# One signal of TensorE per half group, and an MLP that runs three groups ahead, in the edge loop of a graph kernel

## The reference

```python
h = silu(edge_feats @ A1 + b1)          # 8 -> 64
h = silu(h @ A2 + b2)                   # 64 -> 64
tpw = h @ A3                            # 64 -> 128, split in w0..w3
ss, vs = s[sender], v[sender]           # rows gathered from a table of the nodes
out_s0 = ss * y_s * w0;  out_s3 = (vs . y_v) / R3 * w3
out_v1 = ss * y_v * w1;  out_v2 = vs * y_s * w2
message = segment_sum(all of these, receiver) / 10
```

## Time and profile before

| what | us |
|---|---|
| median of 3 runs (2710.15 to 2735.73) | 2723.78 |
| the profiled execution | 2727.58 |
| its span on the core | 2725.8 |
| first `by_attributes` to the end of the last MLP wait (1380.98 to 2649.80) | 1268.8 |

### The profile page before, as it was taken

One profiled execution on the slowest core, in us unless ns is written; L12 is line 12 of the kernel. 1 busy time (PEld: TensorE's weight loads), 2 busy tenths in 40 slices (PEclk: granted clock), 3 DMA queues, 4 the chain that ended last, 5 costly groups with the idle time before them and its releaser, 6 DMA issues. The chain is left out here.

```text
span 2725.8 us, 32746 instructions
## 1 busy us (share of the span) xinstructions
PE 2131.8 (78%) x10250; PEld 1643.8 (60%) x10250; DVE 1571.8 (58%) x3518; ACT 1519.3 (56%) x4753; POOL 1585.9 (58%) x1672
## 2 busy tenths in 40 slices
PE   6488888888888888888768767777777777777776
PEld 4467767777776777767645545554554555555555
DVE  5356666666666665666735555554554555555557
ACT  3455454545455555454556656656666666666662
POOL 1666666666666666666166665665665665665660
PEclk8689999999999999898977888888887888888889
DMA  8666666666666666666111111111111111111111
GB/s 304 203 185 201 204 197 175 169 177 174 182 175 179 179 177 169 176 174 181 47 52 46 47 44 44 48 43 45 47 43 43 48 44 46 50 48 40 45 43 48
DMA packets 121049, 309.60 MB, mean 114 GB/s; under 512 B 29058, under 2 KB 42604, under 8 KB 120876
## 3 DMA queue, kind: packets, MB, share of 16 engines
q0 software_dynamic: 93264, 273.00, 36.0%
q1 hardware_dynamic: 27612, 34.51, 3.8%
HBM read 288.14 MB, written 19.26 MB: 113 GB/s over the span
## 5 line engine op out<-in xcount | busy, mean ns | idle before, releaser
L664 POOL DMA_INDIRECT sender<-table,src_index x832 | 785.8, 945 | 539.3 <-issue 286.9
L369 POOL DMA_INDIRECT shared<-gates,seq_index x833 | 789.1, 947 | 502.4 <-issue 221.2
L759 ACT ACTIVATE bank<-bank,attr 128x64 f32<-128x64 f32 x3328 | 702.3, 362 | 3.9 <-issue 3.6
L392 PE MATMUL bank<-ident,shared 128*128 128x128 f32 x3332 | 497.9, 294 | 230.7 <-DVE h_lo L467 155.2
L445 ACT ACTIVATE bank<-bank,bias 128x512 f32<-128x512 f32 (+1 forms) x663 | 401.1, 634 | 494.7 <-PE bank L404 322.9
L392 PEld LDWEIGHTS bank<-ident,shared 128*128 128x128 f32 x3332 | 425.1, 152 | 321.5 <-DVE h_lo L467 187.0
L713 PE MATMUL bank<-msg,select 128*128 128x256 f32 x1664 | 504.0, 455 | 2.1 <-DVE msg L806 2.1
L795 DVE TENSOR_TENSOR side<-sender,bank 128x192 f32<-128x192 f32 x416 | 147.0, 353 | 598.4 <-ACT bank L759 394.1
L698 PEld LDWEIGHTS bank<-a,h 64*128 64x128 f32 x1664 | 238.2, 218 | 378.9 <-issue 255.2
L698 PE MATMUL bank<-a,h 64*128 64x128 f32 x1664 | 281.1, 318 | 196.4 <-ACT bank L759 138.0
L713 PEld LDWEIGHTS bank<-msg,select 128*128 128x128 f32 x1664 | 356.8, 225 | 85.8 <-issue 9.3
(11 more groups left out here) (88 smaller groups left out, 2161.9 us busy)
## 6 DMA issues: line engine op xcount, KB each, us to landing
shared<-gates,seq_index POOLq DMA_INDIRECT x833
sender<-table,src_index POOLq DMA_INDIRECT x832
gates<-shared SPq DMA_DIRECT2D x49, 256.0 KB, 4.0
feats<-attr_in SPq DMA_DIRECT2D x13, 256.0 KB
x<-x_nodes_in SPq DMA_DIRECT2D x12, 256.0 KB
table<-up SPq DMA_DIRECT2D x12, 256.0 KB, 2.3
out<-x SPq DMA_DIRECT2D x12, 256.0 KB
shared<-x_t_in SPq DMA_DIRECT2D x3, 704.0 KB, 10.2
```

What stands on the lines that cost most here:

```text
L369: pool.indirect_dma_start(out=rows[:, k % SLOTS, j, :], out_offset=None, in_=t["gates"], in_offset=bass.IndirectOffsetOnAxis(ap=seq_index[ ...
L392: last = pe.matmul(bank[:, j * P:(j + 1) * P], rows[:, k % SLOTS, j, cols], ident[:], is_transpose=True, start=(j == 0), stop=False, skip_ ...
L664: pool.indirect_dma_start(out=sender[:, hg % 4, j, :], out_offset=None, in_=t["table"], in_offset=bass.IndirectOffsetOnAxis(ap=src_index[: ...
L759: last = act_e.activation(wy[:, j, :, k, :], w[:, 2 * i + j, :, min(k, 1), :], ACT.Copy, scale=attr[:, k, tile:tile + 1])
```

## The change

Six semaphores of PE become one, `e_pe`. PE adds to it once for each product in the lead-in, and once for each half of an iteration in the main loop; the values at which a reader may go on are worked out in four small functions. The MLP layers run three groups ahead in place of two, and `h2` has three buffers for that. The first layer moves behind the sums of its half, as the second one did already. The orders of ACT's loop and the waits of PE stay the same but for the three groups. In the diff below `mlp1`, `mlp2`, `mlp3` and `sum_receivers` return their last product and signal nothing themselves; the first block of changed lines is PE's, the second ACT's. DVE and SP are changed in their waits alone: `summed(hg - RING)` in `selections`, `summed` of the window's last half group in `add_window`, and `first_done(GROUP * (s - 1) - 1)` before a load of features.

```diff
+EARLY = 3
-        h2 = sb("h2", [P, 2, 512])
+        h2 = sb("h2", [P, EARLY, 512])
+        def first_done(g):
+            return 2 * g + 1 if g < EARLY else 2 * g + 2
+        def second_done(g):
+            return 2 * g + 2 if g < EARLY else 2 * g + 3
+        def weights_done(hg):
+            return 2 * EARLY + 1 if hg < 2 else 2 * EARLY + hg
+        def summed(hg):
+            return 2 * EARLY + hg + 3
...
-                    for g in range(2):
-                        mlp1(g)
-                        mlp2(g)
-                        mlp3(g)
+                    for g in range(EARLY):
+                        mlp1(g).then_inc(e_pe, 1)
+                        mlp2(g).then_inc(e_pe, 1)
+                    mlp3(0)
+                    mlp3(1).then_inc(e_pe, 1)
                     for g in range(NGROUP):
-                        mlp1(g + 2)
                         mlp3(2 * g + 2)
-                        sum_receivers(2 * g - 1)
-                        mlp2(g + 2)
+                        last = sum_receivers(2 * g - 1)
+                        last = mlp1(g + EARLY) or last
+                        last.then_inc(e_pe, 1)
                         mlp3(2 * g + 3)
-                        sum_receivers(2 * g)
-                    sum_receivers(NHALF - 1)
+                        last = sum_receivers(2 * g)
+                        last = mlp2(g + EARLY) or last
+                        last.then_inc(e_pe, 1)
+                    sum_receivers(NHALF - 1).then_inc(e_pe, 1)
...
-                        act_e.wait_ge(e_p1, g + 1)
-                        if g >= 2:
-                            act_e.wait_ge(e_p2, g - 1)
+                        act_e.wait_ge(e_pe, first_done(g))
-                        act_e.wait_ge(e_p2, g + 1)
-                        if g >= 2:
-                            act_e.wait_ge(e_w, 2 * (g - 1))
+                        act_e.wait_ge(e_pe, second_done(g))
+                        if g >= EARLY:
+                            act_e.wait_ge(e_pe, weights_done(2 * (g - EARLY) + 1))
-                        act_e.wait_ge(e_w, hg + 1)
+                        act_e.wait_ge(e_pe, weights_done(hg))
                     for g in range(NGROUP):
                         by_attributes(4 * g)
                         by_attributes(4 * g + 1)
-                        silu1(g + 2)
+                        silu1(g + EARLY)
                         by_attributes(4 * g + 2)
                         by_attributes(4 * g + 3)
-                        silu2(g + 2)
+                        silu2(g + EARLY)
```

More of the change, by code:

```diff
@@ L637, in build @@
         e_gather = [sem(f"e_gather{i}") for i in range(4)]
-        e_p1, e_h1, e_p2, e_h2, e_w, e_scaled = (sem(n) for n in ("e_p1", "e_h1", "e_p2", "e_h2", "e_w", "e_scaled"))
-        e_sel, e_msg, e_half, e_acc = (sem(n) for n in ("e_sel", "e_msg", "e_half", "e_acc"))
+        e_pe, e_h1, e_h2, e_scaled = (sem(n) for n in ("e_pe", "e_h1", "e_h2", "e_scaled"))
+        e_sel, e_msg, e_acc = (sem(n) for n in ("e_sel", "e_msg", "e_acc"))
         e_side, e_free, e_next = (sem(n) for n in ("e_side", "e_free", "e_next"))
-        e_sems = [e_rel, e_turn, *e_feats, *e_gather, e_p1, e_h1, e_p2, e_h2, e_w, e_scaled,
-                  e_sel, e_msg, e_half, e_acc, e_side, e_free, e_next]
+        e_sems = [e_rel, e_turn, *e_feats, *e_gather, e_pe, e_h1, e_h2, e_scaled,
+                  e_sel, e_msg, e_acc, e_side, e_free, e_next]
         mlp_bank, weight_bank, scaled_bank, acc_bank = banks[0], banks[1:3], banks[3:5], banks[5:7]
         slot_bank = banks[7][:, 0:P].rearrange("p (j n) -> p j n", j=1)
+        def first_done(g):
[6 more added lines that the diff above has]
+            return 2 * EARLY + hg + 3
         rounds = nc.values_load(rounds_word[0:1, 0:1], min_val=1, max_val=ROUNDS)
@@ L653, in _ @@
                         if s >= 2:
-                            sp.wait_ge(e_p1, GROUP * (s - 1))
+                            sp.wait_ge(e_pe, first_done(GROUP * (s - 1) - 1))
                         sp.dma_start(feats[:, s % 2, :], t["attr8"][s]).then_inc(e_feats[s % 2], 16)
@@ L678, in mlp1 @@
                             pe.wait_ge(e_h2, g)
-                        pe.matmul(mlp_bank[:], a1[:, b * P:(b + 1) * P], feats[:, s % 2, :],
-                                  start=True, stop=True).then_inc(e_p1, 1)
+                        return pe.matmul(mlp_bank[:], a1[:, b * P:(b + 1) * P], feats[:, s % 2, :],
+                                         start=True, stop=True)
                     def mlp2(g):
@@ L685, in mlp2 @@
                         pe.wait_ge(e_h1, g + 1)
-                        pe.matmul(mlp_bank[:], a2[:], h1[:, g % 2, :], start=True, stop=True).then_inc(e_p2, 1)
+                        return pe.matmul(mlp_bank[:], a2[:], h1[:, g % 2, :], start=True, stop=True)
                     def mlp3(hg):
@@ L698, in mlp3 @@
                             last = pe.matmul(weight_bank[hg % 2][:, j * P:(j + 1) * P],
-                                             h2[channels, g % 2, j * P:(j + 1) * P],
+                                             h2[channels, g % EARLY, j * P:(j + 1) * P],
                                              a3[channels, :], start=True, stop=True)
-                        last.then_inc(e_w, 1)
+                        return last
                     def sum_receivers(hg):
@@ L715, in sum_receivers @@
                                              start=(tile in FIRST), stop=(tile in LAST))
-                        last.then_inc(e_half, 1)
-                    for g in range(2):
-                        mlp1(g)
-                        mlp2(g)
-                        mlp3(g)
+                        return last
+                    for g in range(EARLY):
[3 more added lines that the diff above has]
+                    mlp3(1).then_inc(e_pe, 1)
                     for g in range(NGROUP):
-                        mlp1(g + 2)
                         mlp3(2 * g + 2)
-                        sum_receivers(2 * g - 1)
-                        mlp2(g + 2)
+                        last = sum_receivers(2 * g - 1)
+                        last = mlp1(g + EARLY) or last
+                        last.then_inc(e_pe, 1)
                         mlp3(2 * g + 3)
-                        sum_receivers(2 * g)
-                    sum_receivers(NHALF - 1)
+                        last = sum_receivers(2 * g)
+                        last = mlp2(g + EARLY) or last
+                        last.then_inc(e_pe, 1)
+                    sum_receivers(NHALF - 1).then_inc(e_pe, 1)
                 @block.scalar
@@ L743, in silu2 @@
                             return
-                        act_e.wait_ge(e_p2, g + 1)
-                        if g >= 2:
-                            act_e.wait_ge(e_w, 2 * (g - 1))
-                        act_e.activation(h2[:, g % 2, :], mlp_bank[:], ACT.Silu, bias=b12[:, 1:2]).then_inc(e_h2, 1)
+                        act_e.wait_ge(e_pe, second_done(g))
+                        if g >= EARLY:
+                            act_e.wait_ge(e_pe, weights_done(2 * (g - EARLY) + 1))
+                        act_e.activation(h2[:, g % EARLY, :], mlp_bank[:], ACT.Silu, bias=b12[:, 1:2]).then_inc(e_h2, 1)
                     def by_attributes(pair):
@@ L782, in selections @@
                         if hg >= RING:
-                            dve.wait_ge(e_half, hg - RING + 1)
+                            dve.wait_ge(e_pe, summed(hg - RING))
                         dve.tensor_tensor(select[:, hg % RING], slot_bank.to_broadcast([P, HALF, P]),
@@ L811, in add_window @@
                         block, turn = divmod(start, P)
-                        dve.wait_ge(e_half, int(WINDOWS[i][-1]) // HALF + 1)
+                        dve.wait_ge(e_pe, summed(int(WINDOWS[i][-1]) // HALF))
                         if i:
```

## The result

The changed kernel takes 3542.77 us (median of 4 runs, 3537.26 to 3544.88) beside 2729.76 us before: slower, ratio 1.301 with a 95% interval of 1.293 to 1.308. The profiled execution took 3542.16 us, its span is 3540.4 us.

The account below looks back on a forecast made before the run. The prediction took handing over between PE and ACT as the bound. 202 turns of 10.26 us replace 1268.8 us, + 803.7, with the ends + 818.7: some 3543 us on the median of 2723.78, range 3450 to 3718.

Parts of the forecast that it names:

- The bound read from the profile: Main edge loop, 1269 us: no engine full; ACT waits 464.8 us for two MLP layers, 2.28 us a half group.
- Part 1, fewer signals: Edge loop: six PE signals a group become two, worth part of 464.8 us at most; page estimate 11 us.
- Part 2, the turns: Edge loop: PE's mlp3 waits for ACT's by_attributes, ACT's next silu for PE's signal behind it, so both take turns.
- Part 3, the length of a turn: Edge loop: ACT 3.94, handing over 0.09, PE's burst 6.23 (median of eleven), a turn 10.26 us against 6.22.
- Part 4, signals in the new loop: Edge loop: POOL pauses in each turn, so lateness is costed at nothing, with 0.3 us as upper end.
- Part 5, the ends: Lead-in with a third group + 8 us, the last three groups + 7 us.
- the clock stays up: Rival: PE's bursts in the edge loop run at full clock, a turn 7.97 us, time 3080; 6 in 100.
- signals stay late: Rival: PE's signals in the edge loop cost 2.28 us more a turn, 12.54 us, time 4003; 8 in 100.
- the lateness goes: Rival: turns do not bind, ACT's idle time in the edge loop falls, at most 306 us less, 2418; 3 in 100.

Follow-up runs that it names:

- two signals alone: Kernel before with its own order, two TensorE signals a group in place of six: 2785.39 us against 2800.79; on another chip 2271.14 us, ratio 1.0002.
- order alone: Changed kernel's order and three groups ahead, but with the six signals of the kernel before: 3333.99 us, ratio 1.469; changed kernel on that kind of chip 3335.44.
- fillers: Changed kernel with four unused products added after each layer: 2884.2 and 2883.4 us, beside 3335.44 us for the changed kernel.

## Why the prediction was right

*The bound read from the profile* held: ACT waited to be handed its layers, and no engine was full. On the late chips most of that waiting was for late signals, as the semaphore records and the 36 us without gathers show.

*Part 1, fewer signals*: costed at nothing but for a rival. The two signals alone are 0.3% below before on the late chip, with nothing inside the interval, and 0.02% above it on the prompt one. By the Trainium skill, page "TensorE: Matmul & The Clock Gate", section "The cost: per-tile semaphore tail", an increment costs about 26 ns, which was 11 us for the four that are dropped (an estimate from that page). Those 11 us are 0.4% and lie within the interval of the late chip's pair; the prompt chip's pair hides them behind the gathers. The turns show none of them, 10.24 us with six signals and with two, where two increments less in a turn would be 0.05 us by that figure. The prediction says that the trace disagrees with the page "in both directions"; that reading was wrong, since 0.04 us and 4.6 us both lie above 26 ns and only the second is far from it.

*Part 2, the turns*: shown by the timelines above, and by the order alone, which has the same time as the whole change. The description of the change says that the first layer moves behind the sums of its half "as the second one did already". In the diff the second layer moves too, from ahead of `mlp3(2g+3)` to behind it and `sum_receivers(2g)`. The prediction used both moves; they were not tried one by one.

*Part 3, the length of a turn*: 10.26 us forecast, 10.24 us measured (1391.99 to 3450.58 us, 201 turns). ACT's idle time is 6.30 us a turn (1266.3 / 201), 6.3 forecast; PE's burst is 1239.0 / 201 = 6.16 us in this stretch, against the median of 6.23 in the earlier trace rows. The mean of those eleven, 6.54, would have given 63 us more in all, still inside the range; that the median came so close is partly luck. The granted clock was forecast below 0.7 and was 0.70. The floor of a turn with the clock up, a rival at 7.97 us, was measured at 8.01 with fillers. In the changed kernel itself this rival did not happen.

*Part 4, signals in the new loop*: in the turns shown a silu starts 0.04 us after its product, and POOL pauses before every half group:

```profile
POOL sender L680 <- DVE msg L823: 1116.5, 202, 5.9
```

The reason I gave was half of the truth. That lateness belongs to long runs of gathers held on the late chip (no gathers, no lateness, and the table above). That it belongs to gathers alone did not: on the prompt chip they run without pause and every signal is prompt. The prediction's 1.30 is therefore that of the late chip. On the prompt one the same change takes 1.47 times as long, since the kernel before had no lateness to lose. The 3335 us there lie outside the range of 3450 to 3718. The time came out right because the changed kernel was measured on a chip like that of the rows, which is luck as far as the prediction goes.

*Part 5, the ends*: forecast + 15 us, measured + 19.5, and split otherwise. From PE's first layer to the first `by_attributes` it is 19.6 us in place of 13.3, + 6.3 where 8 was forecast. From the first activation behind the last `silu2` to the first one of the second layer norm it is 34.3 us in place of 21.1, + 13.2 where 7 was forecast. There ACT waits 2.3 to 2.7 us three times, as far as the profile shows for messages and sums, which the prediction had left out. The turns give 2066.8 - 1268.8 = 798.0 us where 803.7 was forecast, and the stages ahead were 2.9 us shorter. All in all + 818.7 was forecast on the profiled execution; it is 3542.16 - 2727.58 = 814.6. Errors of a few us in each part cancelled.

*The rivals*: the clock stays up, signals stay late, and the lateness goes, all fell. The last one's condition, a layer that is done while ACT still scales, was never met: PE idled before each `mlp3`.

## What to carry to other kernels

When a wait is moved to a signal that stands for several products, list what each product in front of the signal waits for itself; if one of them waits for the work that the waiting engine has just done, the two engines take turns, and no distance in groups helps. A loop of turns pays twice, once for the overlap that goes (here at least 1765 - 1269 = 496 us, 2.4 us a half group, in which both engines worked) and once for the clock, which falls in every pause (2.23 us of 10.24). Before a count of signals is cut, look whether a signal is late at all and beside what.

## What the runs showed of the hardware

- One and the same kernel takes 2266 to 2272 us on two chips and 2710 to 2808 us on others. On those two a reader starts about 0.04 us after TensorE's product. On the others a signal of TensorE arrives microseconds late (4.6 us in the earlier trace rows, and ScalarE waited up to 13.1 us for one) when the product ends 7.5 us or more into a run of gathers (212 of 214 signals). It arrives at once when GpSimd pauses some 5 us after every four (none of 165 late) or issues none (none of 610). What differs between the chips, and by what way gathers hold up a signal, the runs don't show.
- On a chip of the late kind, an order with each layer earlier had longer runs of gathers (3.2 half groups in place of 2.3) and was 2.8% slower.
- Products that nothing uses, put in TensorE's pauses, made a kernel 452 us faster (3335 to 2883): the granted clock went from 0.69 to 1.00, and the same burst from 6.2 to 3.9 us.
